# Moving rounding and a cast of the edge records from VectorE to ScalarE in a graph network's setup

## The reference

```python
agg   = segment_sum(x[src], dst)                          # block 0: then two products and a residual
mean  = segment_sum(x[src], dst) / max(deg, 1)            # block 1: twice
neigh = zeros.at[dst].add(norm[:, None] * (x @ Wphi.T)[src])   # block 2: four steps, weighted by edge_weight
out   = relu(segment_sum((x @ W + b)[src] + edge_attr @ We + be, dst))   # block 3
x = layernorm(x + block(x))                               # after each block
```

## Time and profile before

| quantity | us |
|---|---|
| median of three runs | 1142.05 |
| profiled execution, its own time | 1141.16 |
| span of that execution (first to last instruction) | 1139.4 |
| PE busy | 1037.4 (91%) |
| DVE busy | 526.9 (46%) |
| ACT busy | 288.2 (25%) |

### The profile page before, as it was taken

One profiled execution on the slowest core, in us unless ns is written; L12 is line 12 of the kernel. 1 busy time (PEld: TensorE's weight loads), 2 busy tenths in 40 slices (PEclk: granted clock), 3 DMA queues, 4 the chain that ended last, 5 costly groups with the idle time before them and its releaser, 6 DMA issues.

```text
span 1139.4 us, 25123 instructions
## 1 busy us (share of the span) xinstructions
PE 1037.4 (91%) x10553; PEld 633.4 (56%) x10553; DVE 526.9 (46%) x936; ACT 288.2 (25%) x595; POOL 55.1 (5%) x69
## 2 busy tenths in 40 slices
PE   1348889888889999999999999999999999999997
PEld 1246777777645655544557444574445744457455
DVE  6987989995433346522232222232222324444333
ACT  1466898887520000000000000000000002112100
POOL 4610000000000000000000000000000000000000
PEclk9557999998999999999999999999999999999999
DMA  8236677667895874877749876498765897745931
GB/s 253 64 31 265 278 302 328 282 285 290 324 417 214 326 292 165 343 293 283 271 149 409 322 312 242 183 372 334 304 253 208 336 367 268 272 172 216 411 132 32
DMA packets 55783, 301.96 MB, mean 265 GB/s; under 512 B 6880, under 2 KB 10354, under 8 KB 52147
## 3 DMA queue, kind: packets, MB, share of 16 engines
q1 hardware_dynamic: 50224, 290.54, 65.8%
q0 software_dynamic: 3344, 9.67, 2.8%
q10 hardware_dynamic: 2160, 0.98, 0.4%
HBM read 235.93 MB, written 65.26 MB: 264 GB/s over the span
## 4 chain that ended last, share of the span: by engine, by line
PE 75%; DMA 13%; DVE 5%; ACT 3%; issue 2%; SPq 1%; POOL 0%; ACTq 0%; DVEq 0%
PE ps L1298 46%; PE ps L1291 17%; DMA weight_mats<-arena 12%; PE ps L1253 4%; PE ps L1208 2%; PE ps L1379 2%; PE ps L1266 2%; PE ps L1406 1%; ACT arena L1047 1%; DVE arena L687 1%; DMA arena<-edge_table,ptr 1%; ACT arena L1045 1%; ACT x_buf L1102 1%; PE ps L1235 0%; DMA edge_table<-arena 0%
## 5 line engine op out<-in xcount | busy, mean ns | idle before, releaser
L1298 PE MATMUL ps<-arena,parts_even 125*128 125x500 f32 (+2 forms) x700 | 267.5, 537 | 0.0
L1298 PE MATMUL ps<-arena 125*128 125x500 f32 (+2 forms) x700 | 267.5, 537 | 0.0
L1298 PEld LDWEIGHTS ps<-arena,parts_even 125*128 125x128 f32 x700 | 129.4, 188 | 120.6 <-issue 106.7
L1298 PEld LDWEIGHTS ps<-arena 125*128 125x128 f32 x700 | 129.3, 188 | 120.5 <-issue 106.7
L1031 ACT ACTIVATE XT<-ps 128x500 f32<-128x500 f32 (+2 forms) x49 | 26.5, 541 | 492.3 <-PE ps L1266 492.3
L1291 PE MATMUL ps<-arena 125*128 125x500 f16 (+3 forms) x700 | 139.4, 352 | 1.7 <-DVE arena L733 1.3
L1045 ACT ACTIVATE arena<-ps 128x400 f16<-128x400 f32 (+1 forms) x195 | 129.6, 665 | 35.5 <-PE ps L1406 23.6
L1406 PE MATMUL ps<-arena 64*128 64x52 f16 (+1 forms) x6500 | 105.4, 181 | 35.8 <-DVE arena L687 28.6
L1406 PEld LDWEIGHTS ps<-arena 64*128 64x128 f16 x6500 | 96.0, 96 | 53.3 <-ACT arena L1047 34.1
L687 DVE TENSOR_TENSOR arena<-arena 128x4224 f16<-128x4224 f16 (+2 forms) x52 | 115.2, 2237 | 21.9 <-PE ps L1406 21.9
L1047 ACT ACTIVATE arena<-ps 128x400 f32<-128x400 f32 (+1 forms) x195 | 122.2, 626 | 0.0
(11 more groups left out here) (184 smaller groups left out, 722.6 us busy)
## 6 DMA issues: line engine op xcount, KB each, us to landing
arena<-weight_mats SPq DMA_DIRECT2D x20, 3250.0 KB, 11.7
arena<-weight_mats SPq DMA_DIRECT2D x20, 3000.0 KB, 10.6
arena<-count_mats SPq DMA_DIRECT2D x15, 3125.0 KB, 15.1
weight_mats<-arena SPq DMA_DIRECT2D x13, 3125.0 KB, 14.6
count_mats<-arena SPq DMA_DIRECT2D x13, 1562.5 KB, 6.2
arena<-weight_mats SPq DMA_DIRECT2D x4, 2437.5 KB, 8.7
arena<-weight_mats SPq DMA_DIRECT2D x4, 2250.0 KB, 8.5
arena<-count_mats SPq DMA_DIRECT2D x3, 2343.8 KB, 9.5
```

Source lines behind the costliest of these rows:

```text
L1298: ins = t.matmul(o, xs[:, k, :], rhs, start=(k == 0), stop=(k == NC - 1))
```

## The change

Three things are altered, all in the setup.

- ACT gets its own `records(i)`: two activations compute source / 25 plus the rounding number, and subtract that number again (`rec_hi_ok`), and a third casts the masked weight to `w1` (`w1_ok`). The calls stand in ACT's queue behind the `XT` copies and between the other copies. `hi32` has two buffers.
- DVE's `records(i)` loses lines 608, 610 and 611 of the old kernel. It waits for `rec_hi_ok` before `lo32` and for `w1_ok` before `w2`. Both reductions now stand ahead of `w2`, and `rec_ok` is raised by an instruction of its own behind it.
- The table holds both indices less 12 (`MID`), so that rounding to nearest gives the floor. The copy that writes them becomes a `tensor_scalar` with an add. POOL makes the matching constant `dmid` and two columns for the rounding number.

```diff
-            v.tensor_copy(t_rows[:, :, 0:2], t_pairs)
+            v.tensor_scalar(t_rows[:, :, 0:2], t_pairs, -float(MID), None, ALU.add)
...
                 v.tensor_tensor(cnt, sdw[0:NP, cs, :, 1], d_c[:, cs].to_broadcast([NP, n, SLOTS]), ALU.is_equal)
-                link(v.tensor_scalar(hi32[:, 0:n, :], source, 1.0 / NC, -0.5 + 0.5 / NC, ALU.mult, ALU.add))
-                v.tensor_tensor(wm, weight, cnt, ALU.mult)
-                link(v.tensor_scalar(hi, hi32[:, 0:n, :], ROUND_MAGIC, -ROUND_MAGIC, ALU.add, ALU.add))
-                v.tensor_copy(w1, wm[:, :, 0:last])
+                dve.wait_ge(rec_hi_ok, i + 1)
                 link(v.scalar_tensor_tensor(lo32[:, 0:n, :], hi, -float(NC), source, ALU.mult, ALU.add))
+                v.tensor_tensor(wm, weight, cnt, ALU.mult).then_inc(wm_ok, 1)
                 v.tensor_reduce(S8[:, cs, 0], cnt, AX, ALU.add)
-                v.scalar_tensor_tensor(lo, lo32[:, 0:n, :], 1.0, cnt[:, :, 0:last], ALU.add, ALU.mult)
-                v.tensor_tensor(w2, wm[:, :, 0:last], w1, ALU.subtract).then_inc(rec_ok, 1)
-                link(v.tensor_reduce(S8[:, cs, 1], wm, AX, ALU.add))
+                v.scalar_tensor_tensor(lo, lo32[:, 0:n, :], float(MID + 1), cnt[:, :, 0:last], ALU.add, ALU.mult)
+                dve.wait_ge(wm_ok, i + 1)
+                v.tensor_reduce(S8[:, cs, 1], wm, AX, ALU.add)
+                dve.wait_ge(w1_ok, i + 1)
+                link(v.tensor_tensor(w2, wm[:, :, 0:last], w1, ALU.subtract))
+                dve.sem_inc(rec_ok, 1)
...
+            def records(i):
+
+                cs, n = slice(REC_AT[i], REC_AT[i + 1]), REC_AT[i + 1] - REC_AT[i]
+                whole = hi32[i % 2][:, 0:n, :]
+                act.wait_ge(sd_in[i], 16 * n)
+                s.activation(whole, sdw[0:NP, cs, 0:SLOTS - 1, 0], ACT.Identity, bias=magic_col[0:NP, 0:1],
+                             scale=1.0 / NC).then_inc(rec_hi_chain, 1)
+                act.wait_ge(rec_hi_chain, i + 1)
+                s.activation(hiR[:, cs, 0:SLOTS - 1], whole, ACT.Identity, bias=magic_col[0:NP, 1:2]).then_inc(rec_hi_ok, 1)
+                act.wait_ge(wm_ok, i + 1)
+                s.activation(w1R[:, cs, 0:SLOTS - 1], w_slots[:, cs, 0:SLOTS - 1], ACT.Copy).then_inc(w1_ok, 1)
+
             for g in range(GROUPS):
...
+            records(0)
             act.wait_ge(x_in, 32)
             s.activation(parts_even[:, 0], Xn[:, :, :], ACT.Copy, scale=X_SCALE).then_inc(round_ok, 1)
...
+            records(1)
+            records(2)
             for b in range(4):
                 record_columns(b)
+            records(3)
...
             for b in range(4, 8):
                 record_columns(b)
+            records(4)
             act.wait_ge(fold_ps, 1)
             s.activation(L1_W[0][:, :], ps[:, 5, 0:D], ACT.Copy)
             s.activation(L1_W[1][:, :], ps[:, 5, D:2 * D], ACT.Copy).then_inc(fold_copied, 1)
+            records(5)
```

More of the change, by code:

```diff
@@ L78 @@
 ROUND_MAGIC = 1.5 * 2 ** 23
+MID = NC // 2
 def chunks_of(g):
@@ L132, in build_program @@
         dval = sb("dval", [128, FINDS * FIND])
+        dmid = sb("dmid", [128, NC])
+        magic_col = sb("magic_col", [128, 2])
         eps_col = sb("eps_col", [128, 1])
@@ L201, in build_program @@
         REC_MAX = max(z - a for a, z in zip(REC_AT, REC_AT[1:]))
-        hi32 = at(106400, NP, [REC_MAX, SLOTS - 1])
+        hi32 = [at(o, NP, [REC_MAX, SLOTS - 1]) for o in (106400, 112664)]
         lo32 = at(111400, NP, [REC_MAX, SLOTS - 1])
@@ L297, in build_program @@
         fold_copied = sem("fold_copied")
+        rec_hi_chain = sem("rec_hi_chain")
+        rec_hi_ok = sem("rec_hi_ok")
+        wm_ok = sem("wm_ok")
+        w1_ok = sem("w1_ok")
         fold_ps = sem("fold_ps")
@@ L472, in _ @@
                            allow_small_or_imprecise_dtypes=True)
+            nc.gpsimd.iota(dmid[:, :], [[1, NC]], base=-MID, channel_multiplier=NC,
+                           allow_small_or_imprecise_dtypes=True)
+            nc.gpsimd.memset(magic_col[:, 0:1], ROUND_MAGIC)
+            nc.gpsimd.memset(magic_col[:, 1:2], -ROUND_MAGIC)
             nc.gpsimd.iota(win[:, WIN:], [[1, FINDS * FIND]], base=0, channel_multiplier=NC,
@@ L552, in _ @@
                 v.tensor_scalar(before[:, a], node_no, blk_firstf[:, a:a + 1], None, ALU.is_gt).then_inc(before_ok, 1)
-            d_c = dval[0:NP, 0:NC].unsqueeze(2)
+            d_c = dmid[0:NP, :].unsqueeze(2)
             dve.wait_ge(first_ps, 1)
```

## The result

The changed kernel took 1149.17 us in the median (1146.72 to 1151.51, four runs), the kernel before 1141.59 us (1140.84 to 1144.28, four runs). The ratio is 1.0056 with a 95% interval of 1.0039 to 1.0073, so it is slower by 6.4 us (4.5 to 8.3). The profiled execution took 1146.72 us with a span of 1144.9, which is 5.6 us above the profiled execution of before. A second set of six runs gave 1149.76 against 1143.51 and a ratio of 1.0053 (1.0037 to 1.0069).

A forecast was written before the change was run, and what follows sets the result against it. Setup, limited by DVE, was taken to delay the write-bound pair stage one for one: waits 5.6 + 2.5 + 1.6 + 2.4, less 7.3, plus 0.5 gave +5.3, clock -0.6, so +4.7 on 1142.05: 1146.8 us, range 1143.3 to 1149.4.

The forecast's parts named there:

- The range's top, 1149.4: Upper end of the forecast: slower table `tensor_scalar`, plus ACT slower by 0.1 us in each of the 18 activations.
- What bounds it: 107 to 300 us: two 14.8 us writes per pair, period 16.16; DVE limits setup, whose delay passes one for one.
- The waits: In the setup, DVE waits for ACT's `hi` 5.6, 2.5, 0, 1.6, 2.4 and 0 us in calls 0 to 5.
- What VectorE loses: In the setup's six calls, 18 instructions taken off DVE gain 7.3 us if DVE never waits.
- `rec_ok` behind the reductions: In each setup call a reduction and the semaphore instruction now stand around `w2`, so PE waits 0.5 us for `rec_ok`.
- ScalarE's pace: Setup activations take 0.842 ns an element plus 0.167 us; rounding steps 0.42, 0.52 or 0.47 us with their bias.
- Side edits at 0: In the setup, the table's `tensor_scalar` and POOL's three new fills cost 0; bounds for the table 0 and +0.8 us.
- The clock's -0.6 us: From 71 to 107 us, the later start shifts PE's clock level; a quarter of a possible 2.6 us gain.
- ScalarE in time everywhere: Rival: in the setup ACT never keeps DVE waiting, so 1135.3 us, faster; chance 0.05.
- The clock giving 2.6 us back: Rival: between 71 and 107 us PE's clock rises earlier, giving +2.7 us, 1144.8, inside 0.3%; chance 0.2.
- The slower pace of the table's `tensor_scalar`: Rival: in the setup the table write from int32 takes 1.8 us, adding 0.8 us, 1147.6; chance 0.15.

The follow-up runs named there:

- every rounding early: Changed kernel with every rounding placed ahead in ScalarE's queue and casts where VectorE will have their input: 1140.27 us against 1143.38 for the kernel before, ratio 0.9965.
- the side edits alone: Changed kernel keeping the table less 12, its `tensor_scalar` and GpSimd's constants, with VectorE rounding and casting again: 1143.89 us, ratio 1.0003 against the kernel before.

## Why the prediction was right

It named the direction, the mechanism and the places. Its 1146.8 us stands against a median of 1149.17, inside its range. The size was low: +4.7 us forecast, +6.4 and +6.1 measured. And that the measured median is inside the range has some luck in it. The range's top, 1149.4, adds 0.1 us for each of ScalarE's 18 activations, while the bounds of the same prediction let only nine of them delay VectorE; by that count the top is 1148.5, and the median lies above it. By its steps:

- **What bounds it.** Right. The first long write moved by 6.3 us, the period stayed at 16.2 us, and the end moved by 5.5. In the profiled executions the 5.5 are 5.7 of the setup and 0.6 up to the first long write, less 0.5 in the build behind it and 0.3 in the rounds; the last two vary by more than that between executions.
- **The waits.** Forecast 5.6, 2.5, 0, 1.6, 2.4 and 0 us for the six calls; measured 5.20, 2.50, 0, 1.69, 2.46 and 0. The first is shorter because in that profile the seven copies end 0.47 us earlier than in the one of before. In the second profile it was 5.54. That ScalarE's order alone makes these waits is shown by the three experiments that change only the order.
- **What VectorE loses.** Mis-sized. I took 7.3 us from the durations of 18 instructions. Without their waits for ScalarE the six calls are shorter by 1.01, 0.80, 1.27, 1.39, 1.11 and 0.78 us, 6.4 in sum. Most of the difference is a hand-over that I had not counted in every call. Before, a call's last instruction was followed by the wait for its own completion, with 0.03 to 0.13 us of idle time. Now a semaphore instruction stands there too, and the idle time is 0.15 to 0.22 us behind each of the six calls (the timeline prints three of them). That is 0.7 us in sum. The other 0.3 us is the overlap with the neighbour, some 0.08 us, which is lost ahead of each of the four waits.
- **`rec_ok` behind the reductions.** Forecast 0.5 us, measured 0.3: the batch of TensorE starts 0.03 us ahead of the flags (65.88 and 65.91) where it started 0.30 ahead (60.15 and 60.45). So 11.85 - 6.36 + 0.27 = 5.8, less 0.05 for the earlier start, is the 5.7 of the trace. The forecast sum was 5.3, and the setup's real delay lies 0.4 us above it: 0.9 us less gain, against 0.25 us less waiting and 0.2 us less here.
- **ScalarE's pace.** A little low. The first rounding step takes 717 ns for 315 elements and I said 520. The second takes 560. It costs up to 0.2 us at a wait. At call 0 the earlier end of the copies covered it, and at calls 3 and 4 the waits came out 0.1 us longer than forecast.
- **Side edits at 0.** Right, shown by the experiment.
- **The clock's -0.6 us.** The term itself came true in the profiled execution, and what it left out was larger. TensorE worked for some 9.0 us at the lower level (90.51 to 96.0 and 102.72 to 106.2, by windows of 1 us), where it had worked for 10.6, and the work ahead of its pause and the work between the pause and the next wait took 0.2 and 0.4 us less. But the pause was 4.60 us and not 3.39, so the stretch up to the first long write grew by 0.56 us beyond the setup's delay. I had taken the pause as fixed. It isn't: in five of the ten profiles the work ahead of the pause takes 7.1 to 7.9 us and the pause 4.0 to 4.8, and the two add up to 11.9 us each time. What the clock gives back ahead of the pause, the pause takes up. Over the other five the sum is 11.2 to 12.5 us, so this is what a run varies by, and no term of the change. It shouldn't have been priced from one trace.
- **The rivals.** ScalarE in time everywhere was refuted for the change. It is what every rounding early comes to, and it gave -4.0 us rather than the -6.8 that I had put on it, because VectorE's calls are shorter by 6.4 us and not 7.3, 1.3 us of waiting stays in calls 0 and 1, and `rec_ok` costs its 0.3: 4.8 us at best. Of that late gathers took 0.7 at call 0 and 0.4 at call 1 in the profile, which leaves the 3.7 that it shows. The clock giving 2.6 us back isn't seen in the medians. The slower pace of the table's `tensor_scalar` was refuted by the side edits alone.

The Trainium skill ("VectorE: DVE Perf Modes", section "Rules for kernel authors") advises to make the count of chained instructions small and not the semaphores. The runs agree with half of it: fewer instructions did make VectorE's calls shorter. But each of the four cross-engine waits was longer than what its call saved (5.20 against 1.01, 2.50 against 0.80, 1.69 against 1.39, 2.46 against 1.11 us), until the other queue was put in order.

## What to carry to other kernels

Before work moves to an engine that is idle on average, look at what stands in its queue at the moment when the result is needed: the queue is worked off in order, and here one wait of 5.2 us at the start cost nearly as much as taking 18 instructions away had saved (6.4 us). Split the moved work by when its input is there and put each piece ahead of whatever is not yet wanted. The same three activations gave +6.1 us in one order and -4.0 us in another. Then ask what the next limit is: here it was the gathers. And where runs of one kernel spread over 5 us, look for the stretch that varies before a term for it goes into a sum.

## What the runs showed that was not expected

- An activation that reads every third f32 element was slower than one that reads them side by side: 717 and 560 ns for 315 elements, 530 and 455 for 189, in the same call with the same kind of bias. The slower one also writes f32 and not f16, but that doesn't explain it: a copy from PSUM that writes 500 f32 elements takes 587 ns in the same trace. It also has a scale other than 1. No run changed the step alone, so that the step makes the difference isn't shown.

```profile
L997 ACT ACTIVATE arena<-arena,magic_col 125x315 f32<-125x315 f32 x3 | 2.2, 717 | 0.0
...
L1000 ACT ACTIVATE arena<-arena,magic_col 125x315 f16<-125x315 f32 x3 | 1.7, 560 | 0.1
```

- TensorE's pause in the first pass of the loop over pairs was 3.39, 4.60, 5.06, 4.78, 4.03, 4.72, 2.99, 4.70, 4.78 and 4.78 us in the ten profiles. The timeline names no releaser. The DMA view has a trace of one: in every profile one packet of the queue that it calls `instruction` falls into the pause, at 93.6 to 93.8 us before and at 100.2 to 100.4 after, and the pause ends some 2.2 to 2.5 us behind it in all ten (the packet is placed to 0.2 us). Later packets of that queue have no such pause beside them. The rows are those of 93 to 94 us before and of 100 to 101 us after.

```profile
q8 instruction: 1, 0.02, 5.9%
```

```profile
q8 instruction: 1, 0.02, 5.9%
```

This fits a TensorE that waits for its next instructions while SP's first pair of matrices is being written. No run tried it, so it isn't shown.
